# Reordering a software-pipelined gated delta rule attention: the four engines' order strings of a fused adaLN block

## What is computed

```python
mixed = silu(causal_conv4(x @ W_qkvz.T))            # k, q, v0, v1; two more columns are the gates z
q, k = l2norm(q), l2norm(k)
decay = tril(exp(g[i] - g[j]))                       # g: cumulated log gates of a chunk
A = -strict_tril(k_beta @ k.T * decay)
T = inverse(eye - A)
for chunk in chunks:                                 # the scan over a state of 128 x 128 per value head
    v_new = T @ v_beta - (T @ k_beta_exp_g) @ state
    out = (q * exp(g)) @ state + (q @ k.T * decay) @ v_new
    state = state * exp(g_last) + (k * exp(g_last - g)).T @ v_new
y += (rms_norm(out) * norm_w * silu(z)) @ W_out.T
```

## Time and profile before

| | |
|---|---|
| three runs, median (lowest to highest) | 4832.42 us (4830.36 to 4836.11) |
| profiled execution, first to last instruction | 4831.3 us (its own time around that span is not listed) |
| TensorE busy | 97% of the span |
| VectorE busy | 91% |
| ScalarE busy | 72% |
| GpSimd busy | 57% |
| DMA, mean over 16 engines | a quarter of the span |

### The profile page before, as it was taken

How to read it: one execution, slowest core, us unless ns; L and a number is a source line. 1 busy time by engine, 2 the same in 40 slices (tenths; PEclk the granted TensorE clock), 3 DMA queues, 4 the chain that set the end, 5 groups by cost and what they waited for, 6 DMA issues and landing times. The chain is left out here.

```text
span 4831.3 us, 132942 instructions
## 1 busy us (share of the span) xinstructions
PE 4671.0 (97%) x38533; PEld 3195.1 (66%) x38788; DVE 4411.5 (91%) x9152; ACT 3467.6 (72%) x8336; POOL 2743.0 (57%) x2329
## 2 busy tenths in 40 slices
PE   5899999999999999999999999999999999999978
PEld 3566666666666666666666666666666666666643
DVE  4899999999999999999999999999999999999953
ACT  3677777777777777777777777777777777777732
POOL 2456665656565665656566665656566665656520
PEclk7999999999999999999999999999999999999988
DMA  4222222222222222222222222222222222222122
GB/s 156 65 75 79 68 86 70 88 66 87 67 79 79 68 86 71 88 66 87 67 80 79 68 86 66 92 66 84 70 78 80 66 87 66 92 66 84 55 79 83
DMA packets 185165, 377.26 MB, mean 78 GB/s; under 512 B 86400, under 2 KB 95744, under 8 KB 184960
## 3 DMA queue, kind: packets, MB, share of 16 engines
q1 hardware_dynamic: 185088, 376.46, 24.7%
HBM read 360.13 MB, written 16.25 MB: 78 GB/s over the span
## 5 line engine op out<-in xcount | busy, mean ns | idle before, releaser
L658 PE MATMUL p_proj<-hid,w_in 128*128 128x512 f32 x3072 | 1626.7, 612 | 30.0 <-POOL ident_h L1185 28.9
L1018 DVE SCALAR_TENSOR_TENSOR conv<-p_proj,taps,conv 128x509 f32<-128x509 f32 (+2 forms) x1536 | 1134.8, 739 | 48.2 <-ACT conv L886 34.9
L1199 POOL TENSOR_TENSOR root<-sums,half_pow 128x8 f32<-128x8 f32 x128 | 210.8, 1647 | 862.9 <-DVE sums L1028 843.9
L1225 POOL TENSOR_SCALAR_AFFINE_SELECT x_bd<-x_t 128x512 bf16<-128x512 bf16 x640 | 422.6, 660 | 213.5 <-DVE x_t L1102 211.2
L658 PEld LDWEIGHTS p_proj<-hid,w_in 128*128 128x128 f32 x3072 | 497.3, 192 | 55.1 <-POOL ident_h L1185 29.1
L1093 DVE TENSOR_TENSOR y_h<-p_lev,y_h 128x512 bf16<-128x512 f32 x640 | 440.2, 688 | 74.4 <-PE p_lev L725 74.4
L868 PE MATMUL p_out<-h_t,w_out 128*128 128x512 f32 x1024 | 476.5, 608 | 2.2 <-DVE h_t L1164 1.1
L936 ACT ACTIVATE x_bd<-x_t 64x512 bf16<-64x512 bf16 x640 | 397.7, 621 | 96.3 <-DVE x_t L1102 96.2
L1102 DVE STREAM_TRANSPOSE x_t<-y_h 128x512 bf16<-128x512 bf16 x640 | 450.3, 704 | 4.5
L1072 DVE SCALAR_TENSOR_TENSOR ga<-p_out,neg_c,dec 128x256 f32<-128x256 f32 x1024 | 412.9, 477 | 35.4 <-ACT dec L924 34.8
L886 ACT ACTIVATE conv<-p_proj,taps 128x512 f32<-128x512 f32 x512 | 351.7, 687 | 121.9 <-PE p_proj L658 119.3
(11 more groups left out here) (213 smaller groups left out, 12562.4 us busy)
## 6 DMA issues: line engine op xcount, KB each, us to landing
w_in<-in_w_in SPq DMA_DIRECT2D x128, 768.0 KB, 6.3
g_row<-rows_scratch SPq DMA_DIRECT2D x128, 512.0 KB, 3.2
hid<-h_scratch SPq DMA_DIRECT2D x128, 512.0 KB, 7.4
e_row<-exp_rows_scratch SPq DMA_DIRECT2D x128, 512.0 KB, 5.3
w_out<-in_w_out SPq DMA_DIRECT2D x128, 256.5 KB, 2.7
x<-in_x SPq DMA_DIRECT2D x8, 512.0 KB, 10.6
h_scratch<-x SPq DMA_DIRECT2D x8, 512.0 KB, 2.6
y_scratch<-y_acc SPq DMA_DIRECT2D x8, 512.0 KB, 6.1
```

Of the source, the lines that this page charges most:

```text
L658: last = pe.matmul(p_proj[tile % 2][:], w_in[p][:, kt, tile * P:(tile + 1) * P], hid[p][:, kt, :], start=(kt == 0), stop=(kt == KT - 1))
L1018: dve.scalar_tensor_tensor(conv[:, tile, late:], p_proj[tile % 2][:, 0:S - late], taps[p][:, tile, j:j + 1], conv[:, tile, late:], ALU.mul ...
L1225: pool.affine_select(x_bd[:, :, HB:P], x_t[:], [[0, U], [0, HB]], ALU.is_ge, zero, base=-HB, channel_multiplier=1).then_inc(s["xbd_low"], 1)
```

## The change

It rewrites the four order strings; tasks, instructions, tiles and waits stay as they are.

```diff
-PE_ORDER = ("M2@3 ON1@1 O0@2 VT0@3 Y2@3 KS1@2 W1@2 M3@3 TR1@2 P0@4 Y3@3 U1@2 P1@4 M4@3 KS2@2 O1@2 P2@4 Y4@3 TR2@2 "
-            "P3@4 M5@3 VT1@3 O2@2 U2@2 P4@4 KS3@2 Y5@3 P5@4 KT@4 QT@4 XD@3 Q6@3 TR3@2 P6@4 Z6@3 P7@4 D0@3 O3@2 XC@3 "
-            "D1@3 KK0@4 KK1@4 P8@4 OY0@1 OY1@1 G0@3 L@4 P9@4 W0@3 M1@4 P10@4 TR0@3 Y1@4 G1@3 P11@4 U0@3 ON0@2")
-ACT_ORDER = ("GE@2 OT3@0 C3@2 OQ3@0 XC@1 SV0@2 AO@2 v0@1 IV0@1 XB1@2 VX0@1 v1@1 SV1@2 XB2@2 OT0@1 Z0@2 Z1@2 XB3@2 "
-             "IV1@1 VK0@2 VX1@1 C0@3 XB4@2 OT1@1 OQ0@1 VX2@1 C1@3 OQ1@1 XB5@2 OT2@1 VK1@2 OQ2@1 SK@3 SQ@3 C2@3 KN@3 "
-             "QN@3 XD@2 VX3@1 KT@3 YC@2")
-DVE_ORDER = ("T10@3 y0@3 T11@3 X1@3 q1@3 YA1@0 VW0@2 y1@3 X2@3 ST0@2 HT0@1 q2@3 HT1@1 y2@3 RR1@2 X3@3 q3@3 VW1@2 "
-             "y3@3 ST1@2 X4@3 q4@3 T0@4 RR2@2 T1@4 y4@3 VW2@2 X5@3 T2@4 q5@3 T3@4 ST2@2 T4@4 T5@4 y5@3 SN1@3 s11@3 "
-             "s10@3 RR3@2 T6@4 p6@3 KN@4 QN@4 T7@4 T8@4 SN2@3 F0@3 SM0@4 SM1@4 SM2@4 SM3@4 F1@3 SN0@3 GA0@4 GA1@4 "
-             "GA2@4 GA3@4 T9@4 YA0@1 OS0@2 AB0@4 AB1@4 OS1@2")
-POOL_ORDER = ("SL@3 OP@1 XB1@3 ON@1 XB2@3 SD1@2 GL@4 XB3@3 QD@3 XB4@3 AR@3 SD2@2 AL@3 XB5@3 PW@4 RL@3")
+PE_ORDER = ("O0@2 ON1@1 M2@3 P11@3 VT0@3 Y2@3 KS1@2 W1@2 M3@3 TR1@2 P0@4 Y3@3 U1@2 P1@4 M4@3 KS2@2 P2@4 Y4@3 O1@2 P3@4 M5@3 "
+            "TR2@2 VT1@3 P4@4 U2@2 P5@4 KS3@2 Y5@3 O2@2 KT@4 QT@4 XD@3 Q6@3 TR3@2 P6@4 Z6@3 P7@4 D0@3 XC@3 D1@3 O3@2 KK0@4 "
+            "KK1@4 P8@4 OY0@1 OY1@1 G0@3 L@4 P9@4 W0@3 M1@4 P10@4 TR0@3 ON0@2 G1@3 Y1@4 U0@3")
+ACT_ORDER = ("GE@2 OT3@0 C3@2 OQ2@0 OQ3@0 SV0@2 XC@1 v0@1 IV0@1 XB1@2 VX0@1 v1@1 SV1@2 OT0@1 XB2@2 Z0@2 XB3@2 OQ0@1 VX1@1 IV1@1 "
+             "Z1@2 C0@3 XB4@2 AO@2 OT1@1 OQ1@1 C1@3 VK0@2 VK1@2 XB5@2 VX2@1 C2@3 SK@3 SQ@3 OT2@1 KN@3 KT@3 XD@2 VX3@1 QN@3 YC@2")
+DVE_ORDER = ("VW0@2 HT0@1 y1@3 X2@3 ST0@2 q2@3 HT1@1 y2@3 RR1@2 X3@3 SN1@3 q3@3 VW1@2 SN2@3 SN0@3 y3@3 ST1@2 X4@3 q4@3 T0@4 "
+             "T1@4 y4@3 RR2@2 T2@4 q5@3 VW2@2 X5@3 T3@4 ST2@2 T4@4 T5@4 y5@3 s11@3 s10@3 RR3@2 T6@4 p6@3 KN@4 T7@4 QN@4 F0@3 "
+             "T8@4 SM0@4 SM1@4 SM2@4 SM3@4 F1@3 GA0@4 GA1@4 GA2@4 GA3@4 OS0@2 T9@4 YA0@1 OS1@2 AB0@4 AB1@4 T10@4 y0@4 T11@4 "
+             "YA1@1 X1@4 q1@4")
+POOL_ORDER = ("SL@3 OP@1 ON@1 XB1@3 GL@4 XB2@3 AR@3 XB3@3 SD1@2 XB4@3 SD2@2 AL@3 QD@3 XB5@3 PW@4 RL@3")
```

## The result

The changed kernel takes **4850.22 us** (median of 8 runs, 4847.58 to 4850.97). Beside it, on the same chip, the kernel before took 4834.84 (8 runs, 4830.36 to 4838.57): ratio 1.0032, 95% interval 1.0022 to 1.0042, so slower by 15 us (0.3%) where 52 were forecast. The profiled execution spans 4848.0 us (4849.8 in all). In the changed kernel a task's line is one lower than before: PW is L1198, and so on.

What follows compares the result with a forecast made beforehand. The prediction took a loop cycle across engines as the bound, with PW's round trip from QN to SM0 deciding F1. Terms 0.52 + 0.05 - 0.09 - 0.06 = +0.42 us, times 124 = 52 us, gave 4884 us; range 4800 to 4920.

Steps and rivals of the forecast that it cites:

- KN to F1: VectorE's stretch with the round trip to PW on GpSimd: 4.79 us against 4.27, so +0.52 an iteration.
- Slack: Where OY waits for GA in the second iteration, the first 0.17 of F1's lateness is free: -0.09 as a mean.
- From F1 round to y3, otherwise nothing: Rest of the loop after F1: the other reorderings change nothing in sum; q2, Y2, y2 and X3 stay put.
- g_exp: GpSimd's SD1 behind XB3, and SyncE's loads starting earlier, keep this load's wait from XB3: -0.06 an iteration.
- SN0 against SD1: Before y3, VectorE's SN0 and GpSimd's SD1 exclude each other on SBUF access: y3 later, +0.05 an iteration.
- AB1 against OP: Rival: GpSimd's OP takes the shared access, making VectorE's AB1 and L 1.6 us late: 5030 us, chance 0.05.
- GE is the bound: Rival: GE by way of GA0, not PW, bounds the loop; relief on ScalarE comes through: 4799 us, chance 0.24.
- P11 behind M2 is taken up by Y2's wait for q2: On TensorE, moving P11 behind M2 costs nothing, since Y2 waits for q2 anyway.

Runs made afterwards that it cites:

- Run 1: Changed kernel with VectorE's QN put back ahead of T7: 4805.10 us, ratio 0.9940.
- run 2: Kernel before with only T7 moved ahead of QN and T8 behind F0 on VectorE: 4868.43 us, ratio 1.0066.
- Run 4: Kernel before with only the changed order between GA3 and q2 (the new front) on VectorE, TensorE and GpSimd: 4805.76 us, ratio 0.9941.
- run 6: Kernel before with the new front (changed order between GA3 and q2), but YA1 left behind q1: 4818.87 us, ratio 0.9969.
- run 5: Kernel before with only GpSimd's SD1 moved behind XB3: 4827.60 us, ratio 0.9987.
- run 14: Changed kernel with YA1 put back behind q1 instead of ahead of X1: 4849.43 us, ratio 1.0033.
- run 3: Changed kernel with VectorE's SN2 and SN0 moved ahead of q3, before SD1 starts: 4851.33 us, ratio 1.0035.
- run 8: Kernel before with the new front (changed order between GA3 and q2), plus ScalarE's OQ2 moved behind C3, out of the stretch before GE: 4807.26 us.
- run 15: Kernel before with the new front (changed order between GA3 and q2), plus T7 ahead of QN and T8 behind F0: 4842.16 us, ratio 1.0015.
- run 9: Kernel before with VectorE's string turned so the loop body begins at VW0 instead of T10: 4840.90 us, ratio 1.0014.

## Why the prediction was right and wrong

- **KN to F1** was right: KN to T7 0.72 (0.71), T7 to QN 0.67 (0.66), QN to PW 0.90, SM0 behind PW's end, F1 4.81 after KN (4.79). Run 1 shows that this is the cause: without it the change is a gain. (The 2.83 us that T7, T8, SN2 and F0 are said to fill include QN's own 0.71; the four fill 2.12. Nothing rests on it.)
- **Slack, "There the first 0.17 of lateness costs nothing: -0.09 as a mean"**, is the first step that failed. I looked for slack only where TensorE waited for GA at OY. The gap before GA0 was slack as well: GA0 came only 0.19 later against KN, 0.24 earlier against OY. Of that q2 kept 0.13 and y3 0.17; 0.11 went where YA0 now waits for OY0 (T9 to YA0 is 0.81 in run 2's trace, 0.70 before). Run 2 puts the slack at 0.29 and the net price at +35 us in place of 53. In the changed order, where the other parts have used some of it, the table leaves 0.10 (QN first against changed: F1 to OY 0.02, OY to y3 0.08), near the 0.09 by another way; there the late root costs its 45 us (run 1), and the larger error is the next step's.
- **"From F1 round to y3, otherwise nothing"**, with "q2, Y2, y2 and X3 fall where they did", is the second, and the larger one. The same tasks in another order are not the same time: VW0 to q2 shrank from 3.07 to 2.76, because two waits of 0.2 without a bracket went. Run 4 prices the front at -28 us. Half of it is there without YA1's move (run 6); the other half needs the earlier loads, so that a late g_exp doesn't hold y3.
- **g_exp**, -0.06: run 5 measures -5 us, -0.04 an iteration. In the old order with the new front the same late load is worth 14 us (runs 4 and 6), though SD1 waits for it 6 times there and not 57: the wait is rare, but in the iteration that run 6 names it holds y3 by 0.9. In the changed kernel SD1's place covers it (run 14), so it isn't to be counted twice.
- **SN0 against SD1**, +0.05: the collision was forecast, and came to SN2. Behind it stands the line of SN2 over the whole run of the changed kernel; before it was 157/160/171.

```profile
L1059 DVE TENSOR_SCALAR q_s<-inv x128: 315/565/567, 152.9 to 4626.4; 128x4 f32<-128x4 f32 x128
```

  SN2 starts at 1527.42 and ends with SD1, at 1527.96 (GpSimd's timeline of the changed kernel):

```profile
1527.35 0.61 POOL L1238 TENSOR_TENSOR state_dec<-state,g_exp 128x256 f32<-128x256 f32 x1
```

  It costs nothing in the whole (run 3). That a one-input VectorE operation is held is what the Trainium skill (SBUF — State Buffer, Who interferes with whom) says of `tensor_scalar` in a two-port mode; these rows agree.
- **AB1 against OP** (rival, 0.05) didn't come: in the changed kernel AB takes 410/422/425 ns, against 408/422/426, so the hold for the whole of OP on which this rival rested isn't there. OP does run beside AB0 (from 1515.48, AB0 from 1515.30) and takes 0.1 more than the 1636/1652/1652 it took before:

```profile
L1243 POOL TENSOR_TENSOR o_sc<-o_sc,neg_half x128: 1635/1747/1854, 211.4 to 4667.6; 128x8 f32<-128x8 f32 x128
```

- **GE is the bound** (rival, 4799) was wrong as a mechanism: in the changed kernel SM0 waits for PW in all 57 iterations and GA0 for GE in none. That run 1's 4805 lies in its range is chance. With QN first VectorE still waits for GE in one iteration of two, and run 8 shows that OQ2, whose move was to bring GE forward, doesn't set its place.

The sum by the runs: +35 for the late root and -28 for the front make +7 (run 15). The changed kernel is at +15. The remaining 8 us belong to the other parts, which cost nothing while QN is first (runs 1 and 4, 4805.10 and 4805.76). So the late root costs 45 us with them and 35 without. By the table they have two effects while QN is first: F1 to OY is 0.09 shorter (2.66, 2.75), and KN to F1 0.07 longer (4.34, 4.27). With the root late both are gone (2.64 and 2.63, 4.81 and 4.81): the slack behind F1 had been spent.

What is left against run 15 is OY to y2, 11.82 against 11.71, of which y3 to KN gives back 0.06. 0.04 of it lies before q2, where VW0 waits for TR0, up to 0.33 in one iteration of two. The rest lies between q2 and y2, and as I read the trace TensorE's order makes it: P11 now stands behind M2, and Y2 follows VT0 with no pause, 0.26 after q2's end (q2 starts at 1523.15 and ends at 1523.83). TensorE's timeline of the changed kernel:

```profile
1522.47 0.40 PE L717 MATMUL p_lev<-y_h,a_bd 128*128 128x64 bf16 x8
1522.71 1.10 PE L657 MATMUL p_proj<-hid,w_in 128*128 128x512 f32 x2
1523.65 0.60 PE L705 MATMUL p_out<-consts,v_t 128*128 128x128 f32 x4
1524.09 0.40 PE L724 MATMUL p_lev<-q_h,x_bd 128*128 128x64 bf16 x8
```

In the kernel before Y2 starts 0.15 after q2's end, in run 15 0.18 in the mean. So the prediction's "P11 behind M2 is taken up by Y2's wait for q2" was short by 0.1. No run moved P11 or TR0 alone; what these 8 us would be without them stays open.

## What to carry to other kernels

Before a small reduction, a slow round trip to another engine and its consumer, send the last input first and fill the trip with work that has no one waiting: here one task moved past another cost or gave 35 to 45 us, more than the 29 us of the rest of the rewrite of four orders. When you price lateness in a loop, look for slack at every wait that the late task shares, and not only at the first, and compare distances between starts with the tasks' own shortest distance: what is over may be a wait without a bracket. Before you take one part of such a change back, look for what the other engines' orders have built on it: three of the runs met such a tie for 110 to 150 us.

## What the runs showed of the hardware that I had not expected

- GpSimd's pow on 8 elements (PW, OP) holds VectorE's operations off far less than its plain operations do. SN2 took 0.16 us inside PW before the change, and 0.56 beside SD1 after it. OP took 0.1 more beside AB0, and AB0 and AB1 took no more beside OP.
- In the kernel before, iterations alternate, 35.22 and 34.95 us from KN to KN (means of the table's stretch; 35.14 and 35.02 from 1500 to 3500), and with them SM0 to F1, 0.75 and 0.93, for the same instructions in the two halves of the loop body. With the seam of VectorE's string turned away (run 9) the 0.93 stayed where it was. What it is, no run shows.
